# Attention over a paged cache: the values' pages loaded by the sync engine instead of gathered by GpSimd

## What is computed

```python
q, k, v = projections of x                     # 32 query heads, 8 key/value heads of 128
q, k = rope(rmsnorm(q)), rope(rmsnorm(k))
kc = k_cache[block_table].reshape(bsz, 512, 8, 128)     # 16 pages of 32 positions per sequence
vc = v_cache[block_table].reshape(bsz, 512, 8, 128)
scores = q @ concat([kc, k]) * SCALE           # masked beyond the sequence's cached length
o = softmax(scores) @ concat([vc, v])
x = x + o @ Wo.T
```

## Time and profile before

| what | us |
|---|---|
| median of 3 runs (lowest to highest) | 2297.32 (2296.19 to 2305.46) |
| the profiled execution's own time | 2293.93 |
| its span, first to last instruction | 2292.3 |
| TensorE busy | 2093.6 (91%) |
| VectorE, ScalarE, GpSimd busy | 1687.3, 1476.6, 1095.0 |
| SP's DMA queue, GpSimd's DMA queue: bytes moved | 371.71 MB, 147.34 MB |

### The profile page before, as it was taken

How to read it: one execution, slowest core, us unless ns; L and a number is a source line. 1 busy time by engine, 2 the same in 40 slices (tenths; PEclk the granted TensorE clock), 3 DMA queues, 4 the chain that set the end, 5 groups by cost and what they waited for, 6 DMA issues and landing times.

```text
span 2292.3 us, 62299 instructions
## 1 busy us (share of the span) xinstructions
PE 2093.6 (91%) x17328; PEld 1365.6 (60%) x17328; DVE 1687.3 (74%) x4445; ACT 1476.6 (64%) x4201; POOL 1095.0 (48%) x1841
## 2 busy tenths in 40 slices
PE   0886999999999958999989999998998998998999
PEld 0443555555555536677767766776776776776775
DVE  7787677777777747777767777776776776776774
ACT  0453667777776746677766766675776776775774
POOL 3343455555556534445444454544444454544442
PEclk9997999999999979999999999999999999999999
DMA  7885465655556579888886887887887887887882
GB/s 281 313 297 201 134 212 171 202 183 192 193 192 206 180 265 323 258 250 251 246 246 207 251 247 214 241 252 212 243 252 214 256 245 219 253 244 215 249 245 68
DMA packets 402162, 522.83 MB, mean 228 GB/s; under 512 B 50865, under 2 KB 297521, under 8 KB 399794
## 3 DMA queue, kind: packets, MB, share of 16 engines
q1 hardware_dynamic: 361010, 371.71, 51.9%
q0 software_dynamic: 40832, 147.34, 19.7%
HBM read 426.36 MB, written 92.54 MB: 226 GB/s over the span
## 4 chain that ended last, share of the span: by engine, by line
PE 52%; issue 4%; SPq 4%; DMA 2%; DVE 1%; POOL 0%; ACT 0%; DVEq 0%; POOLq 0%; ACTq 0%
PE att_scores L1470 13%; PE att_y L1516 13%; PE att_tr L1479 9%; PE att_o L1504 4%; PE att_o L1505 4%; PE att_o L1506 4%; SPq L101 2%; PE att_o L1507 1%; PE att_tr_new L1485 1%; PE att_scores L1471 1%; SPq L95 1%; DMA wh<-k_parts 1%; DMA att_values<-v_parts,att_idx 1%; DVE att_res L1644 0%; DVE att_prob L1615 0%
## 5 line engine op out<-in xcount | busy, mean ns | idle before, releaser
L1615 DVE CUSTOM_DVE_ANT_0 att_prob<-att_scores,att_mask 128x544 f32<-128x544 f32 x512 | 370.7, 724 | 327.6 <-PE att_scores L1471 273.2
L1547 ACT ACTIVATE att_tph<-att_tr 128x512 f16<-128x512 f32 x512 | 306.5, 599 | 369.3 <-PE att_tr L1479 354.6
L1416 POOL CAST att_parts<-wh 128x96 f16<-128x96 f32 x512 | 135.6, 265 | 624.9 <-DVE wh L1632 422.5
L1516 PE MATMUL att_y<-att_wo,att_ot 128*128 128x512 f16 x1536 | 409.3, 380 | 8.7 <-DVE att_res L1644 8.7
L1639 DVE TENSOR_TENSOR att_tpl<-att_tr,att_tph 128x512 f16<-128x512 f32 x512 | 349.8, 683 | 1.1 <-ACT att_tph L1547 0.7
L1479 PE MATMUL att_tr<-ident,wh 128*128 128x128 f32 x2048 | 330.7, 285 | 0.0
L1088 POOL TENSOR_TENSOR proj_rn<-proj_ra,proj_rb 128x512 f32<-128x512 f32 x128 | 189.5, 1481 | 234.9 <-DVE proj_rb L1213 234.9
L964 PE MATMUL proj_blk<-wh,proj_xt 128*128 128x512 f16 x768 | 292.3, 381 | 0.8 <-DVE proj_xt L1169 0.8
L965 PE MATMUL proj_blk<-wl,proj_xt 128*128 128x512 f16 x768 | 292.3, 381 | 0.0
L966 PE MATMUL proj_blk<-wh,proj_xt 128*128 128x512 f16 x768 | 292.1, 380 | 0.0
L1470 PE MATMUL att_scores<-wh 128*128 128x512 f16 x768 | 228.2, 387 | 60.5 <-issue 29.1
(11 more groups left out here) (195 smaller groups left out, 5133.7 us busy)
## 6 DMA issues: line engine op xcount, KB each, us to landing
wh<-k_parts SPq DMA_DIRECT2D x512, 128.0 KB
att_keys<-k_parts SPq DMA_DIRECT2D x512, 128.0 KB
q_parts<-proj_turned SPq DMA_DIRECT2D x128, 256.0 KB, 3.0
v_new_parts<-proj_vp SPq DMA_DIRECT2D x64, 256.0 KB, 3.1
wh<-q_parts SPq DMA_DIRECT2D x32, 512.0 KB
att_query<-q_parts SPq DMA_DIRECT2D x32, 512.0 KB
pro_ring<-in_w_t SPq DMA_DIRECT2D x12, 1024.0 KB
mix_wraw<-in_w_t POOLq DMA_DIRECT2D x24, 512.0 KB, 5.7
```

The lines of the kernel that those rows point to most:

```text
L1516: last = mm(y_ps[:, :], ot[p][:, a, h, :], wo[:, h, w, :], start=(h == 0 and start), stop=(h == HQ - 1 and stop))
L1547: copy = lambda out, in_, **kw: nc.scalar.activation(out, in_, ACT.Copy, **kw)
L1615: v.tensor_tensor_reduce(out=prob[q][:, :], in0=sc[q], in1=mask[bi % 2][:, at:at + LK], scale=1.0, scalar=-3.0e38, op0=ALU.add, op1=ALU.ma ...
```

## The change

The gathers of GpSimd in attention are gone, with the copy of row numbers, its wait and the small tile `idx`. In their place `load_values` stands at the end of SP's `load`: again two loads of 8 page numbers into registers, and 16 DMAs of one page each (32 rows of 4 KB, 128 KB) into a quarter of the partitions of one of the four columns of `values`. The bytes are the same. TensorE waits for 16 DMAs a sample instead of 4. Sample 0 is loaded as before.

```diff
+def load_values(nc, sp, b, values, page_row, v_d, loaded):
+
+    rows = v_d.rearrange("(g s) m -> g s m", s=PS)
+    for half in range(2):
+        _, pages = nc.values_load_multi_w_load_instructions(
+            page_row[0:1, ds(b * NPP + half * (NPP // 2), NPP // 2)], engines=(SP,), min_val=0,
+            max_val=PAGES - 1, skip_runtime_bounds_check_because="page numbers are below PAGES")
+        for j, page in enumerate(pages):
+            c, at = divmod(half * (NPP // 2) + j, LC)
+            sp.dma_start(values[at * PS:(at + 1) * PS, c].rearrange("p h two d -> p (h two d)"),
+                         rows[ds(page, 1)].rearrange("o s m -> (o s) m")).then_inc(loaded, 16)
...
                 after(sp, pv_done, (b - 1) * HK)
                 load_fresh(sp, b, fresh[p], vn_d, vn_in[p])
+                load_values(nc, sp, b, values[p], page_row, v_d, vc_in[p])
...
-            def gather(b, p, c):
-
-                if c == 0:
-
-                    after(pool, pv_done, (b - 1) * HK)
-                    g.tensor_copy(idx[p][:, :], v_idx[:, ds(b * LC, LC)]).then_inc(idx_done, 1)
-                    hold(pool, idx_done, b, idx_seen)
-                g.indirect_dma_start(out=values[p][:, c].rearrange("p h two d -> p (h two d)"),
-                                     out_offset=None, in_=v_d,
-                                     in_offset=bass.IndirectOffsetOnAxis(idx[p][:, c:c + 1], 0)
-                                     ).then_inc(vc_in[p], 16)
...
-
-                    bi, c = i // HK + 1, i % HK - (HK - LC)
-                    if c >= 0 and (bi < BT or not (isinstance(t, int) and t == NT - 1)):
-                        gather(t * BT + bi, bi % 2, c)
...
-                    after(pe, vc_in[p], LC * 16 * (t * (BT // 2) + bi // 2 + p))
+                    after(pe, vc_in[p], NPP * 16 * (t * (BT // 2) + bi // 2 + p))
```

More of the change, by code:

```diff
@@ L1279, in attention @@
         query = [query0, sb("query1", [P, HK, 2, P], F16)]
-        idx = [sb(f"idx{i}", [P, LC], U32) for i in range(2)]
         iota = sb("iota", [P, L], F16)
@@ L1307, in attention @@
         stored = [sem(f"stored{i}") for i in range(2)]
-        idx_done, idx_seen, qk_seen = sem("idx"), sem("idx_seen"), sem("scores_seen")
+        qk_seen = sem("scores_seen")
         mask_done, qk_done, max_done, nb_done, exp_done = (sem(s) for s in (
```

## The result

The changed kernel takes 2600.36 us (median of 4 runs, 2591.14 to 2606.09) against 2296.76 us (4 runs): a ratio of 1.131, 95% interval 1.1265 to 1.1356. The profiled execution has a span of 2601.2 us.

What follows compares the result with a forecast made beforehand. TensorE bounds before at 21.0 us a sample, SP afterwards at 27.5 (16.6 + 10.9). From 843.5 us, 63 samples, tile extras and jumps end SP at 2645.6; landing and the last sample give 2697 us, +17%, range 2560 to 2800.

Steps and rivals of the forecast that it cites:

- What bounds the kernel now: Attention before the change: TensorE bounds at 21.0 us a sample; SP, off the path, has 4.5 us to spare.
- The value page's price: SP's 16 added value pages and two register loads cost 10.9 us a sample, priced like key pages; lower end 8.9.
- SP's own part before that: SP's existing issues per sample before the added value loads, taken as 16.4 us, plus the first tile's extras.
- The steps between samples: On SP: 0.2 us register work a sample, six loop jumps of 5.9 us, and residual loads and result stores per tile.
- The sum: SP's loads from 843.5 us, 63 samples at 27.5 us plus extras, end at 2645.6; landing and last sample give 2697.
- What is removed: GpSimd loses 252 gathers, 244 us of its 1095; it had room, so this was taken as worth nothing.
- Where TensorE waits: TensorE stops some 5 us mid-sample for the values before the first weighing, and little for the keys.
- The clock: After each stop TensorE's half clock costs 2.8 us, making 23.8 us a sample, hidden below SP's 27.5.
- Rival (b): TensorE's half clock decides: 31.5 us a sample in attention, 2945 us; chance 0.08, shared with any other cost on top.
- Rival (a): SP's added issues stay hidden at 0.19 us a page and late gathers go: 2284 us, 0.6% faster; chance 0.03.
- the rule of the Trainium skill: Spreading DMAs over issuing engines saves only usually small sequencer time, so moving gathers to SP costs next to nothing; no change 0.04.
- Rival (c): DMA engines had held SP's issues back; without gathers pages get cheaper: 25 us a sample, 2540 us; chance 0.05.

## Why the prediction was right, point by point

- **What bounds the kernel now** and SP's spare time: right. The run with eight pages, at 22.6 us a sample, lies just beyond the point where the 4.5 us are used up.
- **SP becomes the bound and never waits**: right (0.3 us of waits; 27.1 us a sample on the mean in the loop, 27.5 forecast), and the clearest runs are the two that keep one of count and bytes and change the other.
- **The value page's price**: the mechanism right, the size too high. Forecast 10.9 us a sample, with 10.7 up to the last page's end; measured 634.2 us for 63 samples, 10.07 each. I took the key page's price over that of line 108. The value page is dearer than line 108's 0.46 and cheaper than the key page: 316 ns in the instruction against 333, and 9.34 us for 16 on the mean against 9.65. This is 40 us of the 87 us by which SP finished early.
- **SP's own part before that**, taken at 16.4 us from one stretch: 1018.1 us for 63 samples with the first tile's extras, forecast 1049.9. 32 us. It is 15.8 us in the median sample. From a sample's first issue to the end of the row scales there are 3.2 us in the median sample in place of 3.5. This is not the gathers' doing, since the run with pages beside the gathers has 3.1 us. It goes with SP never waiting: without values and with four wide DMAs, where SP waits again, it is 3.4 and 3.8 us. Why was not tested.
- **The steps between samples**, jumps and tile ends included: forecast 78.1 us, measured 61.4. I read 5.9 us for SP's jump from a kernel whose DMA engines are full at that place (share 0.96 behind the jump, 0.46 in the changed kernel); it was 3.6. But the changed kernel with four tiles a round shows that a jump costs 7.3 to 8.7 us, more than half of it outside the pause, so this term was too low for a jump as a whole, and the others above hold the rest.
- **The sum**: -40 - 32 - 17, with rounding -88 us, and the start 1 us later: SP's last issue ends 87 us early. All three terms erred the same way, which is why the time lies in the lower part of the range. From there the forecast holds: 2.8 us to landing (3 forecast) and 40.3 us to the end; the 3 us for half clock were not needed. The price of 63 us for each us of SP's period is what connects a miss of 1.4 us a sample with 90 us.
- **What is removed**: put at nothing, and that was wrong where TensorE bounds: 22 us without the gathers and their bytes, 12 us with the bytes on SP's queue. In the changed kernel SP is the bound, and TensorE's share of it cannot be seen.
- **Where TensorE waits**: half right. I put one stop of 5 us at the values and little at the keys; there are two of 2 to 3 us each. The step that failed is the distance from the first scores to the first weighing, taken as three steps, 7.9 us. The weighing stands at the end of its step, and in the kernel before the distance is 9.8 us in the median sample of the loop. Here are the two in the trace of the changed kernel, the first scores of a sample and its first weighing (idle time before in brackets):

```profile
1574.71 0.39 PE L1467 MATMUL att_scores<-att_keys,att_query 128*128 128x512 f16 x1 [2.14 <-DMA att_keys<-k_parts]
...
1586.90 0.23 PE L1501 MATMUL att_o<-att_tph,att_values 128*128 128x128 f16 x1 [0.59 <-DMA att_values<-v_parts]
```

12.2 us, 0.6 of them a stop and the rest partly at a lower clock. Against the 9.8 us of the kernel before, the values have 2 us more than I gave them and the keys 2 us less.
- **The clock**: its loss is hidden, as forecast, and smaller than forecast: after a stop of 2.1 us the clock is down for part of the next few us where it was down for 5.6 us after a stop of 3.45. The run with one stop of 5.2 us a sample has 0.91 on the mean where the two short ones leave 0.95, so the two short stops cost less clock. Rival (b) did not occur.
- **Rival (a) and the rule of the Trainium skill** ("DMA: Bandwidth & Descriptors", section "Issuing engines are not separate DMA queues"): the trace disagrees for pages of this size, 0.59 us of issue for 128 KB (9.39 / 16), which the prediction sets against 0.54 us for the transfer. Of its "usually" this kernel is an exception, and 12 issues fewer for the same bytes made the difference of 284 us.
- **Rival (c)** asked whether the DMA engines had held SP's issues up. They had not: with a quarter of the bytes the issue takes the same 316 ns.

## What to carry to other kernels

Count what an engine issues, not only what it computes: an engine that the page shows with no busy time had 4.5 us to spare in 21, and 16 issues of 0.6 us each overdrew it. A gather that issues 128 rows in 1 us of GpSimd's slack is cheap beside four page DMAs of SP, as long as GpSimd has the slack. Where a loop's jump back shows as a standstill on the bounding engine, fewer and longer rounds are worth more than its row says: four jumps fewer saved 36 us in the kernel before, where the row has 4.9 us a jump.

## What the runs showed of the hardware that I had not expected

- An issue on SP costs the same for 32 rows of 1 KB and of 4 KB (316 ns in the instruction) and hardly more for 128 rows of 1 KB (333 ns); with register work and pauses it is 0.59 us for 1 KB or 128 KB a page, and 0.55 us for 512 KB at a fixed address.
- A jump back costs 7.8 to 9.0 us where TensorE bounds and 7.3 to 8.7 where SP does, of which the standstill in the trace is 5 us (TensorE) or 3.6 us (SP). Code of 16 tiles written out ran without such pauses.
- Without gathers TensorE's standstill at the jump is 2.3 us in place of 4.9, also with the same bytes on SP's queue. On either engine the pause at the jump goes with how busy the DMA engines are just behind it: 4.2 to 7.4 us at a share of 0.88 or more, 3.0 to 3.9 us at 0.63 or less, by the table above.
